# A graph attention layer: the preparation ordered anew, R through device memory, half of the projection in plain fp32

## The reference

```python
h  = maximum(layernorm(x), 0)                       # 4096 x 256
h1 = h @ W1 + b1                                    # 4096 x 256
e  = leaky_relu((h1 @ a1)[:, None] + (h1 @ a2)[None, :] + b2, 0.2)
att = softmax(where(adj > 0, e, -1e12), axis=1)     # 4096 x 4096
out = x + elu(att @ h1)
```

## Time and profile before

| what | value |
|---|---|
| median of 3 runs | 437.63 us (437.43 to 437.65) |
| profiled execution | 437.48 us, its span 435.7 us |
| TensorE busy in the span | 412.5 us (95%), 3399 matmuls |
| DVE busy | 377.1 us (87%) |
| ScalarE busy | 315.9 us (73%) |
| POOL busy | 23.0 us (5%) |
| last projection ends, main loop begins | 52.7, 57.7 us |
| last matmul begins, span ends | 431.0, 435.7 us |

### The profile page before, as it was taken

The page is one execution under the profiler, slowest core; times in us unless marked ns, Lnnn a source line. Parts: engine busy times, 40 slices in busy tenths (PEclk is TensorE's granted clock), DMA queues, the critical chain, the costliest instruction groups (busy, mean ns, idle before and its releaser), DMA issues.

```text
span 435.7 us, 8648 instructions
## 1 busy us (share of the span) xinstructions
PE 412.5 (95%) x3399; PEld 409.1 (94%) x3399; DVE 377.1 (87%) x404; ACT 315.9 (73%) x312; POOL 23.0 (5%) x94
## 2 busy tenths in 40 slices
PE   0689979999999999999999999999999999999995
PEld 0688979999999999999999999999999999999995
DVE  3999899999999389999996299999991799999925
ACT  2678899999996298957763798859562989586512
POOL 2333200000000000000000000000000000000003
PEclk9999999999999999999999999999999999999999
DMA  8940015556555725638478155647477256476202
GB/s 271 385 178 1 0 45 211 193 213 211 193 193 194 289 93 205 235 145 261 173 254 308 68 193 200 249 152 263 154 265 259 73 219 213 174 243 238 98 0 98
DMA packets 22360, 80.68 MB, mean 185 GB/s; under 512 B 1472, under 2 KB 14016, under 8 KB 14144
## 3 DMA queue, kind: packets, MB, share of 16 engines
q1 hardware_dynamic: 21920, 79.70, 52.1%
q10 hardware_dynamic: 416, 0.66, 0.5%
HBM read 76.15 MB, written 4.19 MB: 184 GB/s over the span
## 4 chain that ended last, share of the span: by engine, by line
PE 88%; DVE 7%; ACT 2%; DMA 2%; issue 0%; SPq 0%; DVEq 0%; ACTq 0%
PE ps L604 51%; PE ps L606 25%; PE ps L622 2%; PE ps L623 2%; PE ps L624 2%; DVE stats L664 2%; DMA x_s<-x 2%; DVE hnT_lo L691 1%; PE ps L531 1%; DVE h_raw L700 1%; PE ps L533 1%; PE ps L532 1%; DVE xn L681 1%; PE ps L580 1%; PE ps L519 1%; ACT h_raw L439 1%
## 5 line engine op out<-in xcount | busy, mean ns | idle before, releaser
L604 PE MATMUL ps<-hp_hi,w_hi 128*128 (+1 forms) x944 | 229.8, 282 | 0.9 <-ACT w_hi L391 0.9
L606 PE MATMUL ps<-hp_lo,w_hi 128*128 (+1 forms) x944 | 229.7, 282 | 0.0
L738 DVE SCALAR_TENSOR_TENSOR adj_s<-R,p,adj_s 128x1024 f32<-128x1024 f32 x128 | 158.1, 1275 | 31.7 <-ACT adj_s L383 31.7
L604 PEld LDWEIGHTS ps<-hp_hi,w_hi 128*128 128x128 f32 x944 | 178.3, 189 | 1.2 <-ACT w_hi L391 1.1
L606 PEld LDWEIGHTS ps<-hp_lo,w_hi 128*128 128x128 f32 x944 | 178.1, 189 | 0.0
L748 DVE SCALAR_TENSOR_TENSOR w_lo<-adj_s,w_hi 128x2048 fp32r<-128x2048 f32 x64 | 146.0, 2282 | 0.4 <-ACT w_hi L391 0.3
L391 ACT ACTIVATE w_hi<-adj_s 128x2048 fp32r<-128x2048 f32 x64 | 122.4, 1912 | 29.8 <-DVE adj_s L738 29.5
L383 ACT ACTIVATE adj_s<-adj_s 128x2048 f32<-128x2048 int32 x64 | 122.3, 1912 | 23.2 <-DMA adj_s<-adj_t 23.0
L604 PE MATMUL ps<-hp_hi,w_lo 128*128 (+1 forms) x944 | 123.1, 283 | 0.6 <-DVE w_lo L748 0.6
L604 PEld LDWEIGHTS ps<-hp_hi,w_lo 128*128 128x128 f32 x944 | 117.4, 189 | 0.8 <-DVE w_lo L748 0.8
L455 ACT ACTIVATE y<-ps 128x258 f32<-128x258 f32 x24 | 9.3, 387 | 27.9 <-PE ps L624 27.9
(11 more groups left out here) (90 smaller groups left out, 270.2 us busy)
## 6 DMA issues: line engine op xcount, KB each, us to landing
adj_s<-adj_t SPq DMA_DIRECT2D x64, 1024.0 KB, 4.8
x_s<-x SPq DMA_DIRECT2D x8, 512.0 KB, 10.4
o_s<-x SPq DMA_DIRECT2D x3, 1024.0 KB, 7.5
out<-o_s SPq DMA_DIRECT2D x6, 512.0 KB, 6.8
adj_s<-x SPq DMA_DIRECT2D x1, 1024.0 KB, 5.3
out<-adj_s SPq DMA_DIRECT2D x8, 128.0 KB, 1.7
vec<-vectors ACTq DMA_DIRECT2D x1, 384.5 KB, 6.4
W1x<-W ACTq DMA_DIRECT2D x1, 256.0 KB, 4.3
```

Of the source, the lines that this page charges most:

```text
L604: last = pe.matmul(acc, block_w, hh, start=False, stop=False)
L606: pe.matmul(acc, block_w, hl, start=False, stop=False)
L738: last = dve.scalar_tensor_tensor(sgn, R[:, ds(ic * CW, CW)], p[:, ds(source(r, c) + s, 1)], sgn, ALU.max, ALU.mult)
```

## The change

- **Order.** NORM_ACT = 3: ScalarE normalises three tiles of a group and DVE one (two and two in groups 0 and 1). Groups 0 and 1 get mean and variance by bn_aggr on DVE, the others from POOL as before. xn has four buffers. Both lists are written anew: on DVE turn g now holds invert(g+2), normalise(g+2), low_T(g+1), statistics(g+3), keep_h(g); on ScalarE normalise(g+2), relu_T(g+1), root(g+3).
- **Projection.** The first 128 features are projected from split operands (three fp32r matmuls), the other 128 by one plain fp32 matmul. So low_T has one call. The transposes alternate between banks 0, 1 and 6, 7.
- **R.** The column cr is transposed in two parts (8 and 24 tiles) by one TensorE transpose each, ScalarE takes the exponential of the short rows (`exp_r`), SP writes them to device memory and reads them back into all partitions. repeat_s1, spread, keep_s and exp_R are gone.
- **Maximum.** s2 and cr of the last group are read from PSUM by DVE ahead of keep_h(7); the negative sign is in the reduction.
- **Start.** The banks begin with the first matmul itself; the tiny matmul moves to the last pairs (`add_tiny`). The order of low(0,0,0) and mask(0,0,1) is swapped.
- **Loads.** W1 and the vectors are issued by SP behind the first node group; all adjacency tiles come behind the nodes. 32 matmuls on constants run on TensorE while the first nodes load (`keep_warm`).

```diff
-NORM_ACT = 2
+NORM_ACT = 3
+AGG = 2
+WARM = 14
+XN = 4
+R_CUT = CW // P
+R_PART = ((0, R_CUT), (R_CUT, TILES))
...
-EARLY = 6 * GT
+EARLY = 4 * GT
...
-        H0, S0 = 2, 6
+        H0 = 2
+        T0 = (0, 6)
+        RB = (1, 6)
+        GB = 7
...
+            load_nodes(0)
+            sp.dma_start(W1x[:, :, 0:F], W1.rearrange("(c p) f -> p c f", p=P)).then_inc(w_in, 16)
+            sp.dma_start(vec[:, :], vectors.partition_broadcast(P)).then_inc(vec_in, 16)
+            for g in range(1, GROUPS):
                 load_nodes(g)
-                if g == 3:
-                    load_adj(0, 0)
+            load_adj(0, 0)
             for s in range(1, SLOTS):
                 load_adj(s, s)
+            def spread(k):
+                a, b = R_PART[k]
+                tiles = slice(a, b)
+                sp.wait_ge(r_ready, k + 1)
+                sp.dma_start(r_rows[tiles, :], r_row[k][:, :]).then_inc(r_out, 16)
+                sp.wait_ge(r_out, (k + 1) * 16)
+                sp.dma_start(R[:, a * P:b * P],
+                             r_rows[tiles, :].rearrange("t p -> (t p)").partition_broadcast(P)).then_inc(R_in, 16)
+            spread(0)
+            spread(1)
...
-                pool.wait_ge(stat_ready, g + 1)
+                pool.wait_ge(stat_ready, g - AGG + 1)
...
-            for g in range(4):
+            for g in range(AGG, 5):
                 moments(g)
             pool.wait_ge(g3_ready, 1)
-            for g in range(GROUPS):
-                if g + 4 < GROUPS:
-                    moments(g + 4)
+            for g in range(GROUPS - 1):
+                if g + 5 < GROUPS:
+                    moments(g + 5)
                 exponents(g)
+            tiles = slice((GROUPS - 1) * GT, GROUPS * GT)
+            pool.wait_ge(s2_kept, 1)
+            pool.tensor_scalar(cp[:, tiles], s2[:, tiles], -(1 - SLOPE), TOP, ALU.mult, ALU.min).then_inc(c_ready, 1)
...
+            def root_agg(g):
+                act.wait_ge(agg_ready, GT * (g + 1))
+                act.activation(std[:, g * GT:(g + 1) * GT], agg[:, g, :, 1], ACT.Sqrt, bias=eps[:, 0:1]).then_inc(std_ready, 1)
...
+                for t in range(NORM_ACT - (g < AGG)):
...
-                    act.activation(hnT[:, g % 2, kc, :], ps[:, kc, :], ACT.Relu,
+                    act.activation((hnT_hi, hnT_whole)[kc][:, g % 2, :], ps[:, T0[g % 2] + kc, :], ACT.Relu,
...
+            def exp_r(k):
+                act.wait_ge(rT_ready, k + 1)
+                act.activation(r_row[k][:, :], ps[0:R_PART[k][1] - R_PART[k][0], RB[k], 0:P], ACT.Exp).then_inc(r_ready, 1)
...
             act.preload_act_table(ACT.Sqrt)
             act.wait_ge(eps_ready, 1)
-            root(0)
+            root_agg(0)
             normalise(0)
-            root(1)
+            relu_T(0)
+            root_agg(1)
             normalise(1)
-            relu_T(0)
-            sign(0, 0, 0)
-            for g in range(GROUPS):
+            relu_T(1)
+            root(2)
+            normalise(2)
+            root(3)
+            relu_T(2)
+            normalise(3)
+            root(4)
+            for g in range(2, GROUPS):
+                if g + 2 < GROUPS:
+                    normalise(g + 2)
+                if g == 5:
+                    exp_r(0)
+                    act.wait_ge(c_ready, EARLY // GT)
+                    act.activation(p[:, 0:EARLY], cp[:, 0:EARLY], ACT.Exp).then_inc(p_ready, 1)
                 if g + 1 < GROUPS:
                     relu_T(g + 1)
-                if g == 0:
-                    root(2)
-                if g + 2 < GROUPS:
-                    normalise(g + 2)
                 if g + 3 < GROUPS:
                     root(g + 3)
-                if g >= 1:
-                    repeat_s1(g - 1)
+                if g == 3:
+                    sign(0, 0, 0)
                 if g == 6:
-                    act.wait_ge(c_ready, EARLY // GT)
-                    act.activation(p[:, 0:EARLY], cp[:, 0:EARLY], ACT.Exp).then_inc(p_ready, 1)
-                    act.wait_ge(s_kept, CW // (GT * P))
-                    exp_R(0)
-                if g >= 2:
-                    keep_s(g - 2)
-                if g == 7:
+                    sign(0, 0, 1)
                     high(0, 0, 0)
-                if g == 2:
-                    sign(0, 0, 1)
-            repeat_s1(GROUPS - 1)
-            act.activation(p[:, EARLY:TILES], cp[:, EARLY:TILES], ACT.Exp).then_inc(p_ready, 1)
+            exp_r(1)
...
-                    if r is FIRST_ROUND and c == 2 and not last:
-                        exp_R(ic + 1)
...
-            keep_s(GROUPS - 2)
-            keep_s(GROUPS - 1)
-            act.wait_ge(s_kept, GROUPS)
+            act.wait_ge(c_ready, GROUPS)
+            act.activation(p[:, EARLY:TILES], cp[:, EARLY:TILES], ACT.Exp).then_inc(p_ready, 1)
+            act.wait_ge(ones_col, 2)
...
+            def keep_warm(n):
+                for _ in range(n):
+                    pe.matmul(ps[:, H0 + GT - 1, 0:P], ones[:, :], ones[:, :], start=True, stop=True)
+                for cols in (P // 4, P // 2, P):
+                    for _ in range(6):
+                        pe.matmul(ps[:, H0 + GT - 1, 0:cols], ones64[:, :], ones64[:, 0:cols], start=True, stop=True)
...
-                    for kc in range(KC):
-                        pe.matmul(acc, hnT[:, u, kc, node], W_hi[:, kc, :], start=kc == 0, stop=False)
-                        pe.matmul(acc, hnT[:, u, kc, node], W_lo[:, kc, :], start=False, stop=False)
-                        last = pe.matmul(acc, hnT_lo[:, u, kc, node], W_hi[:, kc, :], start=False, stop=kc == KC - 1)
+                    pe.matmul(acc, hnT_hi[:, g % 2, node], W_hi[:, :], start=True, stop=False)
+                    pe.matmul(acc, hnT_hi[:, g % 2, node], W_lo[:, :], start=False, stop=False)
+                    pe.matmul(acc, hnT_lo[:, g % 2, node], W_hi[:, :], start=False, stop=False)
+                    last = pe.matmul(acc, hnT_whole[:, g % 2, node], W1x[:, 1, :], start=False, stop=True)
...
+            def turn_r(k):
+                a, b = R_PART[k]
+                pe.transpose(ps[0:b - a, RB[k], 0:P], cr[:, a:b], ident[:, :]).then_inc(rT_ready, 1)
...
+            pe.wait_ge(h_sum_set, 1)
+            keep_warm(WARM)
+            transposes(0)
+            pe.wait_ge(W_ready, 1)
+            project(0)
+            transposes(1)
+            project(1)
+            transposes(2)
+            for g in range(2, GROUPS):
+                if g + 1 < GROUPS:
+                    transposes(g + 1)
+                if g == 4:
+                    pe.wait_ge(c_ready, R_CUT // GT)
+                    pe.wait_ge(hn_ready, (g + 1) * KC)
+                    turn_r(0)
+                project(g)
+                if g == 4:
+                    pe.wait_ge(r_ready, 1)
...
+            pe.wait_ge(cr_end, 1)
+            turn_r(1)
...
+            def add_tiny(ib):
+                pe.matmul(ps[:, ib, 0:HW], ones64[:, :], h_tiny[:, :], start=False, stop=False)
...
+            def first_tile():
+                pe.wait_ge(hi_ready, 1)
+                pe.wait_ge(hp_tile, 1)
+                pe.wait_ge(hsum_kept, 1)
+                pe.wait_ge(r_ready, 2)
+                for ib in range(BANKS):
+                    if ib == H0:
+                        pe.wait_ge(h_kept, 2 * GROUPS)
+                    pe.matmul(ps[:, ib, 0:HW], w_hi[:, 0, 0, ib * P:(ib + 1) * P], hp_hi[:, 0, :], start=True, stop=False)
+                pe.wait_ge(hp_first, 1)
+                for ib in range(BANKS):
+                    pe.matmul(ps[:, ib, 0:HW], w_hi[:, 0, 0, ib * P:(ib + 1) * P], hp_lo[:, 0, :], start=False, stop=False)
...
+            def aggregate(g):
+                for t in range(GT):
+                    dve.bn_aggr(agg[:, g, t, :], stats[:, g, t, :]).then_inc(agg_ready, 1)
...
+                dve.wait_ge(hn_ready, KC * g + 1)
+                dve.scalar_tensor_tensor(hnT_lo[:, g % 2, :], ps[:, T0[g % 2], :], 0.0, hnT_hi[:, g % 2, :].bitcast(fp32),
+                                         ALU.max, ALU.subtract).then_inc(hn_lo_ready, 1)
...
+            aggregate(0)
             invert(0)
             normalise(0)
             weights()
+            split_weights()
+            low_T(0)
+            statistics(1)
+            aggregate(1)
             invert(1)
             normalise(1)
-            split_weights()
-            low_T(0)
             statistics(2)
+            low_T(1)
+            keep_h(0)
+            statistics(3)
+            invert(2)
+            normalise(2)
+            statistics(4)
+            invert(3)
+            normalise(3)
+            keep_h(1)
+            low_T(2)
             scalars()
-            statistics(3)
-            for g in range(GROUPS):
-                if 0 < g < GROUPS - 2:
+            for g in range(2, GROUPS - 1):
+                if g + 2 < GROUPS:
                     invert(g + 2)
-                if g + 1 < GROUPS:
-                    low_T(g + 1)
-                if g == 0:
```

(51 more changed lines are left out.)

199 lines of the change are left out of this document (79 added, 120 removed).

## The result

The changed kernel takes 449.49 us (median of 4 runs, 448.04 to 452.35) against 437.62 of the kernel before on the same chip: ratio 1.0279, 95% interval 1.0234 to 1.0325. It is slower, as forecast (448.9, range 444 to 453.5). The profiled execution took 448.05 us and its span is 446.3.

A forecast was written before the change was run, and what follows sets the result against it. TensorE's matmul queue bounds the main loop, so its start decides: 437.5 + 8.4 (second pair later) + 1.0 (h_tiny matmuls moved) = 446.9, with 2.0 for the slow clock 448.9 us; range 444 to 453.5.

The forecast's parts named there:

- The ring: Preparation: steps on DVE, POOL and ScalarE each wait for the one before; 6.7 us a turn, 7.9 at g = 3.
- The front: Start of preparation: transposes at 9.3 us, project(0) from 11.9 to 15.1, statistics(5) at 29.3.
- rival D: Start of preparation: weights late, or project(0) at 1.2 GHz, costing 2.7 us; time 451.5; chance 17%.
- The hole before transposes(6): Preparation: TensorE idles some 7.8 us after project(4), waiting for exp_r(0), which ends at 50.8.
- the hole before the transpose of R: Preparation: TensorE idles 4 us before it transposes R.
- The clock: After TensorE's long idleness, transposes(6) and part of project(5) run at the 1.2 GHz level: +2.0 us (1.4 to 3.4, less 0.2).
- R's round trip: R goes to device memory and back over SP's queue, 2.2 + 3.0 us, arriving at 56.0 as keep_h(5) ends at 55.9.
- Rival E: R's way through device memory takes 3 to 4 us longer, moving mask, low_T(7) and project(7); time 452.5; chance 10%.
- The end: End of preparation: first matmul 3.1 us behind the last projection, a gain of 1.9; second pair 8.1 after it, +8.4 overall.
- The tail: Main loop's end: eight h_tiny matmuls of chunk 0 move into the last pair, +1.0 us.
- The shares (rival B): Preparation: engine shares decide, not order; 4.1 us a group on TensorE, time about 428.5; chance 5%.

The follow-up runs named there:

- experiment 3: Changed kernel with 16 dummy matmuls before the transpose of R and 34 before the wait for r_row: 448.21 us.
- experiment 5: Changed kernel run again unedited: 449.58 us; its profiled execution took 450.09.
- experiment 6: Changed kernel with seven dummy matmuls between transposes(0) and the wait for the weights: 448.63 us.
- experiment 7: Changed kernel with exp_r(0) and its table load moved ahead of normalise(7) on ScalarE: 447.61 us.
- experiment 9: Changed kernel without the warming matmuls on constants at its start: 449.89 us.
- experiment 1: Changed kernel with DVE's statistics taken one more group ahead, only the order changed: 444.08 us.
- experiment 8: Changed kernel with the statistics of all eight groups combined by bn_aggr on DVE, none on GpSimd: 447.77 us.
- experiment 10: Changed kernel with statistics two groups ahead, exp_r(0) ahead of normalise(7), and dummy matmuls in the front (9) and the holes (16 and 20): 443.10 us.
- experiment 2: Changed kernel with sign(0,0,0) moved ahead of root(6) in ScalarE's list: 449.77 us.
- Experiment 12: Changed kernel with the preparation's lists reordered by measured landing times, 22 dummy matmuls in the front, 5 behind the broadcast of the maximum: 433.38 us.

## Why the prediction was right, and where it was not

**The ring: right.** Turns forecast at 6.7 and 7.9, measured 6.74 and 7.92, and within 0.01 the same in the traces of experiments 3, 5, 6, 7 and 9, which kept the order of these turns. Experiments 1 and 8 show it as the cause from two sides: one takes the turn's slack back, the other shortens a link. Releasers as forecast: ScalarE before low_T (1.97) and before the reciprocal (0.87).

**The front: sizes off both ways.** Statistics(5) were forecast at 29.3; the first profile has 28.66, the second 30.67. Transposes(0) at 9.35 and project(0) at 11.57 are within 0.4 of the forecast, and that is luck. The nodes landed at 4.33 and not at 5.3, which would have brought the transposes forward by 1 us; but the warming matmuls, which I had through by 9.0, held them up until 9.35. What I had put into rival D with 17%, the vectors late or project(0) at 1.2 GHz, is common: of seven traces of kernels with the changed kernel's front, its warming and no dummies in it, four have a slow project(0), at 4.75 to 4.88 us instead of 3.50, and the vectors are worked on from 7.93 to 8.91. The two together cost 2.0 in experiment 5, where D had 2.7, and can carry the median from 448.05 to 449.5. D's mechanism was right and its chance too small, since I treated it as all or nothing. That the median, 449.49, lies so near to 448.9 is luck in part: the sum was made for an execution without D, which came out 0.85 lower, and I had put the median only 0.15 above it.

**The hole before transposes(6): right in its end, wrong in its length.** Forecast 7.8 us of idleness, measured 5.36. I had the hole before the transpose of R (4 us forecast, 3.84 measured), but I did not count the clock behind it: project(4) ran at half rate (39 to 44 us, clock 0.50), ending at 45.0 instead of some 43. That cost nothing, since exp_r(0) sets the next step, forecast at 50.8 and measured to end at 50.3. In experiment 8 project(4) came without such a hole and ran at the full rate, and there the idleness is 7.26.

**The clock: +2.0 right.** The eight transposes took 1.97 instead of 1.04, and to the mask the slow restart cost 2.0 by experiment 3. That is one pair of traces. From the start of transposes(6) to the mask lie 4.88 us at the upper level (experiments 3 and 10) and, after a slow restart, 6.22 (experiment 7), 6.31 (8), 6.77 (6), 6.79 (9), 6.87 (unedited, twice), 7.36 (2) and 7.73 (1). So it cost 1.3 to 2.9 us, which fits the 1.4 to 3.4, less 0.2 of slack, of the forecast, and it moves a time by more than some of the edits do. The rule that I cited (the Trainium skill, TensorE: Matmul & The Clock Gate, HAM oscillation) holds here, and for shorter holes than I argued with: 3.31 us in experiment 7.

**R's round trip: right.** Forecast to land at 56.0, 0.1 behind keep_h(5) without the clock's share; it landed at 55.4, and the mask started at 57.22, kept by project(5). Rival E did not come about: its 3.8 us are hidden as long as the queue is empty.

**The end: right to about a microsecond.** From the last projection to the first matmul 3.25 (forecast 3.1). First matmul 66.0 + 2.0 of clock = 68.0, measured 67.57. The second pair 9.46 later instead of 8.4 + 2.0 = 10.4. The first pair began at the lower level of the clock (its w_lo block 5.42 behind the first matmul, 3.90 in experiment 8, where the clock was up), and that cost nothing: the second pair waits for w_hi and begins 7.57 behind the first matmul, in experiment 8 7.56. The tail +1.15 instead of +1.0. In sum +10.6 instead of +11.4: the profiled execution is 0.85 under the forecast, of which 0.64 is the front's.

**The shares (rival B): excluded for this order, right for another.** Experiment 12 reaches the 4.1 us a group that I had worked out as TensorE's share, and with it the time falls under that of before. It didn't get to B's 428.5; 4.5 of the 4.9 us between them are the start of project(0), at 16.4 there and not at 11.9.

What stays open: what sets when the clock rises, in the start of an execution and after a hole, and the executions of 450.9 and 452.35, which have no trace. The late vectors and the slow front explain 2 us of them; a fall of the clock in mid-preparation as in experiment 2, or a long slow stretch as in experiment 1, could be the rest, and that is argued, not shown.
